# Attention: scores for the maximum first, scores for the exponentials second, in each half of a unit

## The reference

```python
xn = layernorm(x)
q, k, v = xn @ Wq.T + bq, xn @ Wk.T + bk, xn @ Wv.T + bv      # 16 heads of 8 columns
attn = softmax(einsum('bqhd,bkhd->bhqk', q, k) / sqrt(8))
out = einsum('bhqk,bkhd->bqhd', attn * head_mask, v)
x = x + out @ Wo.T + bo
```

## Time and profile before

| | us |
|---|---|
| median of 3 runs | 2095.73 (2086.49 to 2103.74) |
| the profiled execution | 2100.33 |
| its span | 2098.1 |
| attention, first to last E of it | 647 to 1518, 871 |
| PE busy over the span | 1860.1 (89%) |
| DVE busy | 1496.2 (71%) |
| ACT busy | 1232.2 (59%) |
| POOL busy | 887.4 (42%) |

### The profile page before, as it was taken

The page is one execution under the profiler, slowest core; times in us unless marked ns, Lnnn a source line. Parts: engine busy times, 40 slices in busy tenths (PEclk is TensorE's granted clock), DMA queues, the critical chain, the costliest instruction groups (busy, mean ns, idle before and its releaser), DMA issues. The chain is left out here.

```text
span 2098.1 us, 30450 instructions
## 1 busy us (share of the span) xinstructions
PE 1860.1 (89%) x9600; PEld 1108.9 (53%) x9600; DVE 1496.2 (71%) x2379; ACT 1232.2 (59%) x1914; POOL 887.4 (42%) x875
## 2 busy tenths in 40 slices
PE   3999999999937898999999988888859999999999
PEld 2777777777812333333333333333247777777777
DVE  4767777687517878777787777887447768776775
ACT  3566455555513767666676667776635565556654
POOL 2566555655621222222222222221125565556655
PEclk9999999999955989888888889998879999999999
DMA  2000000000032323222223223222010000000000
GB/s 91 21 11 31 27 24 30 10 30 10 16 59 33 47 47 47 47 42 39 41 44 44 41 41 40 53 44 35 12 36 21 31 11 31 20 30 10 30 14 16
DMA packets 43167, 68.57 MB, mean 33 GB/s; under 512 B 9916, under 2 KB 11444, under 8 KB 43060
## 3 DMA queue, kind: packets, MB, share of 16 engines
q1 hardware_dynamic: 38256, 65.15, 15.7%
q0 software_dynamic: 4096, 1.08, 0.3%
q10 hardware_dynamic: 708, 0.98, 0.1%
HBM read 28.36 MB, written 12.58 MB: 20 GB/s over the span
## 5 line engine op out<-in xcount | busy, mean ns | idle before, releaser
L1259 DVE TENSOR_REDUCE attn_neg_max<-attn_p_score 128x2 f32<-128x1024 f32 x512 | 624.8, 1223 | 211.2 <-PE attn_p_score L941 209.1
L572 POOL TENSOR_TENSOR ffn_hid_low<-ffn_hidden,ffn_hid_high 128x512 fp32r<-128x512 f32 x448 | 580.6, 1298 | 454.9 <-ACT ffn_hid_high L512 454.2
L1096 ACT ACTIVATE attn_exps<-attn_p_score 128x1024 f32<-128x1024 f32 x512 | 519.8, 1025 | 286.6 <-PE attn_p_score L927 284.6
L512 ACT ACTIVATE ffn_hid_high<-ffn_hidden 128x512 fp32r<-128x512 f32 x448 | 281.0, 627 | 255.7 <-DVE ffn_hidden L705 254.8
L503 ACT ACTIVATE ffn_silu<-ffn_p_gate 128x512 f32<-128x512 f32 x448 | 264.0, 589 | 207.8 <-PE ffn_p_gate L375 207.5
L698 DVE TENSOR_TENSOR ffn_gated<-ffn_silu,ffn_p_up 128x512 f32<-128x512 f32 x352 | 240.6, 684 | 175.1 <-PE ffn_p_up L375 112.2
L941 PE MATMUL attn_p_score<-k_pack,q_pack 24*128 24x512 f32 x1024 | 283.2, 553 | 57.7 <-ACT attn_exps L1096 33.0
L958 PE MATMUL attn_p_o<-attn_exps,values 128*32 128x512 f32 x2048 | 312.0, 684 | 8.4 <-ACT attn_o_raw L1102 3.3
L927 PE MATMUL attn_p_score<-q_pack,k_pack 26*128 26x512 f32 x1024 | 271.2, 539 | 14.9 <-DMA q_pack<-attn_max_rows 14.6
L927 PEld LDWEIGHTS attn_p_score<-q_pack,k_pack 26*128 26x128 f32 x1024 | 101.4, 198 | 314.7 <-issue 207.5
L705 DVE TENSOR_TENSOR ffn_hidden<-ffn_gated,ffn_p_spread 128x512 f32<-128x512 f32 x352 | 241.2, 685 | 14.9 <-PE ffn_p_spread L416 4.1
(11 more groups left out here) (146 smaller groups left out, 2220.9 us busy)
## 6 DMA issues: line engine op xcount, KB each, us to landing
q_pack<-attn_q_high SPq DMA_DIRECT2D x128, 64.0 KB
k_pack<-attn_k_high SPq DMA_DIRECT2D x128, 64.0 KB
ffn_x_in<-in_x SPq DMA_DIRECT2D x16, 256.0 KB, 2.8
ffn_x_res<-in_x SPq DMA_DIRECT2D x16, 256.0 KB, 2.8
after_ffn<-ffn_x_out SPq DMA_DIRECT2D x16, 256.0 KB, 2.0
attn_x_in<-after_ffn SPq DMA_DIRECT2D x16, 256.0 KB, 4.6
k_pack<-attn_k_low SPq DMA_DIRECT2D x64, 64.0 KB
q_pack<-attn_q_low SPq DMA_DIRECT2D x64, 64.0 KB
```

Source lines behind the costliest of these rows:

```text
L512: nc.scalar.activation(hid_high[s][0:n, :], hidden[s][0:n, :], ACT.Copy).then_inc(high_ready, 1)
L572: nc.gpsimd.tensor_tensor(hid_low[s][0:n, :], hidden[s][0:n, :], hid_high[s][0:n, :].bitcast(F32), ALU.subtract).then_inc(low_ready, 1)
L1096: nc.scalar.activation(exps[n % len(exps)][:], score_bank("exp", b, n)[:], ACT.Exp, scale=inv_sqrt)\
L1259: V.tensor_reduce(neg_max[g % 2][:, j:j + 2, t], score_bank("max", b, n)[:], AX.X, ALU.max, negate=True).then_inc(max_read, 1)
```

## The change

PE sends M before E in each half. The list `order`, from which the three buffers and their waits follow, has M before E as well. The wait for the packed maxima moves from the head of the unit into `score_exp`, so that only E stands behind it. The other engines do the same operations in the same order; only the buffer numbers that they read change.

```diff
         for k in range(NB):
             for n in range(PAIRS):
-                order.append(("exp", k, n))
                 ahead = k * PAIRS + n + 2 * AHEAD
                 if ahead < NB * PAIRS:
                     order.append(("max", ahead // PAIRS, ahead % PAIRS))
+                order.append(("exp", k, n))
...
                 g, t = divmod(u, NT)
                 n = 2 * u + half
+                if t == 0 and half == 0:
+                    pe.wait_ge(max_packed[g % 2], b.count(MAX_DMA * NQ // 2, MAX_DMA * (g // 2 + 1)))
                 bank_free(pe, "exp", b, n)
...
                 for u in range(UNITS):
-                    if u % NT == 0:
-                        g = u // NT
-                        pe.wait_ge(max_packed[g % 2], b.count(MAX_DMA * NQ // 2, MAX_DMA * (g // 2 + 1)))
...
                     for half in range(2):
-                        score_exp(b, u, half)
                         if there(ahead):
                             score_max(ahead, v, half)
+                        score_exp(b, u, half)
```

## The result

The change makes the kernel slower: 2215.63 us in the median of 4 runs against 2098.44, a ratio of 1.0566 (95% interval 1.0505 to 1.0627). The forecast was 2150, so the sign was right and the loss is more than twice as large. The same kernel in two later sets of runs gave 1.0744 (1.0662 to 1.0827) and 1.0597 (1.0554 to 1.0641); each set is on one chip, with the kernel before beside it.

A forecast was written before the change was run, and what follows sets the result against it. The prediction took a PE-ACT loop of about 3.04 us per attention unit as the bound, moving to DVE at 3.25. Terms +37 and +15 made +52 on 2100.33, or 2152, forecast as 2150; range 2105 to 2210, its own 2115 to 2185.

The forecast's parts named there:

- The loop before: Attention unit before the change: PE waits on ACT's exponential, then PV and the next E(h0); 3.05 us at full clock.
- The loop after: Attention unit after the change: M(h0), DVE's maximum, E(h1), PV; 3.25 us at full clock, 4.71 at the lower.
- Waits of pieces hidden: Pieces' waits for the spare bank and long pieces fit between E(h0) and E(h1); all 1.64 us per batch hidden.
- DVE's side work: Statistics, variance steps and residual on DVE delay maxima in the loop; 0.8 us per full-clock batch, ends 0 and 3.8.
- The DMA wait: E(h0) of unit 4 waits less for the packed maxima; 5 us saved over all batches, ends nothing and 12.
- The sum without the clock: Attention's added time from full-clock batches and lower-clock units, less the DMA saving; +37 us.
- The clock: PE idler in attention, so 50 us more at the lower clock; +15 us, ends none and +44.
- second rival: New loop in attention plus lower clock in most batches twice, DVE's side work in the way; 2185 to 2225, chance 0.23.
- The range: Whole kernel time 2105 to 2210 us, leaving out most of the faster case and the upper end of the clock case.

The follow-up runs named there:

- e8: Kernel before the change, old order, with an unused 128-column ACT copy ahead of the exponential of E(h0); 2179 us, ratio 1.0415.
- e2: Kernel before the change, old order, with an unused 4-column ACT copy ahead of the exponential of E(h0); ratio 1.0163.
- e3: The change, with scores for the maximum of half 1 computed twice in units 15, 0, 1, 5, 9 and 13; 2138 us, ratio 1.0205.
- e18: The change, with scores for the maximum of half 0 computed twice in unit 10, making batches longer; 2226 us, ratio 1.0581.
- e1: The change, with the maximum taken over only 416 of the 512 columns of each head; 2102 us, ratio 1.0059.
- e7: The change, with the maximum taken over only 464 of the 512 columns of each head; 2168 us, ratio 1.0311.
- e9: The change, with scores for the maximum of half 1 computed twice in units 15, 0 and 1 only; 2155 us, ratio 1.0306.
- e12: The change itself run again, unaltered, against the kernel before in a later set; 2246 us, ratio 1.0744.

## Why the prediction was wrong

By its own steps:
- *The loop before*, 3.05 over ACT and PV: right. e8 and e2 lengthened it by their copy and the unit followed.
- *The loop after*, 3.25 and 4.71: right to 0.01, at both levels of the clock. It is where the loss starts.
- *Waits of pieces hidden*: right for units 7, 9 and 11, which take 3.25. Unit 13 takes 3.50.
- *DVE's side work*, 0.8 per batch: present where units 4 and 5 run at full clock (3.52 and 3.60 in batch 9), but they seldom did.
- *The DMA wait*, -5 with -12 as its end: PE's waits for the packed maxima in attention went from 14.6 us to 2.8, so it was the end. The new loop isn't what took them away, though: e3, whose batches begin at full clock, still has 17.7 us of them. The change has hardly any because most of its batches begin at the lower clock.
- *The sum without the clock*, +37: about right. The traces give 32, and e3, whose clock is near that of the kernel before, 44.
- *The clock*, +15, with +44 as its upper end: this is the step that failed. It is +89. I let a fall last 17 us, as in the earlier trace rows, and asked only how many more there would be: 50 us are three more, and five more came. But their mean length also doubled, 13.4 to 26.5 us, which my term did not have in it at all: 17 x 26.5 instead of 12 x 13.4. I had also put PE's busy share in a unit without a piece at 72%, with the 2.33 us of the kernel before, and the trace has 2.17 of 3.25, 67%. The mean clock of attention, 0.75, is under the 0.83 that I had named as the sign of the second rival (the clock goes too, chance 0.23), and that rival's upper end of 2225 held the time. But that is luck: the end was reached with 38 us of DVE's side work, which did not come, and with a clock term of 44, half of what it was.
- *The range*, 2105 to 2210, left that rival's upper part out, and the time of 2215.63 lies there.

In the trace after, from 648 us to the last batch of attention, PE has no idle stretch longer than 1.08 us, and the clock falls 17 times from the second batch to the last but one. The section of the Trainium skill that the prediction set against the change (TensorE: Matmul & The Clock Gate, A second HAM failure mode: psum-queue depth-cycling) says that short idle times of PE between groups of matmuls, which come from cycling through PSUM banks, make the clock swing between its two levels. The trace agrees with it, and it pointed the right way.

Left open: why the new order has 135 us or more at the lower level above the old one at the same loop of 3.25 (e8). The lockstep (e18) doesn't account for it, and M being first cost only some 50 us at 3.05 (e1). The traces have a candidate: the loop may be the same, but PE's idle time in it is not, since M(h1) of the new order runs in part beside E(h0). In unit 15 PE is idle for 0.72 us in the kernel before, 0.82 in e2, 0.88 in e1, 0.92 in e8, 0.97 in e7 and 1.08 in the change, and the times at the lower level, 250 to 281, 305, 302, 429, 464 and 564 to 669, go nearly in that order, whichever of E and M is first. In e3 and e9, with unit 15 filled, it is 0.84 us, and they have 278 and 323. No kernel changed this idle time at an unchanged order and loop without adding work, so it stays an argument. Also open: the same kernel's time at the lower level differs by 100 us between sets of runs (564 and 669).

## What to carry to other kernels

When two consumers drain buffers in turn and the order of filling is swapped, the half of slack moves with it: write down the loop for each buffer, fill, read, release, and what the filling engine must send in between, and put the slack with the slower reader. Where PE waits in each turn of a loop, price the clock as well as the wait: how often it falls, and how long it stays down. Where such a wait can't be removed, useless work in it may pay: here it gave back 77 us of 117 (e3), and 91 of 160 in another set (e9 beside e12).

## What the runs showed of the hardware

- A loop 0.2 us longer per 3.05 cost 32 to 44 us by itself and 89 by the granted clock. The clock fell to the lower of its levels for 496 of 992 us of attention where PE was busy for 2.17 of the 3.25 us of a unit without a piece, and for 209 of 871 us where it was busy for 2.33 of 3.04.
- Once down, the clock didn't come back as soon as PE had no gap: in the trace after it stayed at the lower level from 842.50 to 857.24, units 2 to 4 of batch 3, where PE's records cover all of the 14.74 us.
- Maxima over 832 and 1024 elements last 1024 and 1222 ns (e1 and the change), but two of the longer ones in a row start 1.12 to 1.14 us apart.
- Matmuls on different row strips start together: the two pairs E and M of the earlier trace rows start at 1027.10 and 1027.11 and cost 0.43 us together (to 1027.54), as much as one pair alone (1028.72 to 1029.15).
- Time at the lower level goes with the scatter of one kernel's runs: in the set of e1 the kernel before ran in 2070 us with 178 at the lower level and in 2098 with 285. At 1 - 3.04 / 4.50 = 0.32 each (an estimate from the earlier trace rows), 107 us more are 35, and the difference is 29.
